# Row maxima of a softmax, transposed on their way to DRAM element by element instead of by TensorE and a VectorE copy

## The reference

```
x = x + layernorm(attention(layernorm(x)))
x = x + layernorm(relu(layernorm(x) @ W1 + b1) @ W2 + b2)
attention: scores = (q * 0.25) @ k^T + mask, softmax over the keys, @ v, then the output projection
```

## Time and profile before

| | us |
|---|---|
| median of 3 runs | 2061.07 (2060.56 to 2062.49) |
| profiled execution | 2061.84 |
| its span | 2060.0 |
| TensorE busy | 1938.2 (94%) |
| VectorE busy | 1536.7 (75%) |
| ScalarE busy | 1408.6 (68%) |
| GpSimd busy | 722.8 (35%) |

### The profile page before, as it was taken

The page is one execution under the profiler, slowest core; times in us unless marked ns, Lnnn a source line. Parts: engine busy times, 40 slices in busy tenths (PEclk is TensorE's granted clock), DMA queues, the critical chain, the costliest instruction groups (busy, mean ns, idle before and its releaser), DMA issues. The chain is left out here.

```text
span 2060.0 us, 70899 instructions
## 1 busy us (share of the span) xinstructions
PE 1938.2 (94%) x27904; PEld 1588.0 (77%) x27904; DVE 1536.7 (75%) x2916; ACT 1408.6 (68%) x2341; POOL 722.8 (35%) x905
## 2 busy tenths in 40 slices
PE   3879999999999999999999999999999999999985
PEld 2557887788888778888877888787788878778765
DVE  6577777777787777778777787877778787777631
ACT  2446677777777777777777776777777677777653
POOL 2013333333333333333333333333433334343343
PEclk8789999999999999999999999999999999999998
DMA  4343343334334333433433343343334334333200
GB/s 124 71 84 73 76 90 68 80 80 93 78 81 91 68 79 81 92 78 82 91 67 77 84 90 79 80 91 66 79 84 88 79 82 89 68 80 76 54 27 16
DMA packets 132817, 160.61 MB, mean 78 GB/s; under 512 B 29408, under 2 KB 82400, under 8 KB 132576
## 3 DMA queue, kind: packets, MB, share of 16 engines
q1 hardware_dynamic: 132048, 156.29, 35.8%
q10 hardware_dynamic: 528, 0.52, 0.1%
HBM read 38.21 MB, written 17.83 MB: 27 GB/s over the span
## 5 line engine op out<-in xcount | busy, mean ns | idle before, releaser
L613 DVE TENSOR_REDUCE max_bias<-p_pair 128x4 f32<-128x1024 f32 (+1 forms) x640 | 761.4, 1215 | 104.1 <-PE p_pair L363 87.9
L530 ACT ACTIVATE probs<-p_pair 128x1024 f32<-128x1024 f32 x640 | 638.8, 1027 | 246.4 <-PE p_pair L363 134.9
L746 POOL TENSOR_TENSOR h_lo<-h_f,h_hi 128x512 fp32r<-128x512 f32 x256 | 329.8, 1288 | 477.5 <-ACT h_hi L562 477.4
L366 PE MATMUL p_pair<-stack 49*128 49x256 f32 (+1 forms) x3072 | 352.3, 314 | 36.3 <-ACT probs L530 15.0
L562 ACT ACTIVATE h_f<-p_pair,b_s 128x256 f32<-128x256 f32 x512 | 247.9, 484 | 119.3 <-PE p_pair L393 119.3
L366 PEld LDWEIGHTS p_pair<-stack 49*128 49x128 f32 (+1 forms) x3072 | 241.3, 191 | 111.6 <-ACT probs L530 46.8
L393 PE MATMUL p_pair<-x_hi,w_hi 64*128 64x256 f32 (+1 forms) x2560 | 302.6, 308 | 13.0 <-DVE x_lo L625 5.5
L393 PE MATMUL p_pair<-w_hi,h_hi 64*128 64x256 f32 x2048 | 286.7, 277 | 10.0 <-POOL h_lo L746 7.4
L393 PE MATMUL p_pair<-x_hi,w_lo 64*128 64x256 f32 (+1 forms) x2560 | 295.9, 302 | 0.0
L393 PE MATMUL p_pair<-x_lo,w_hi 64*128 64x256 f32 (+1 forms) x2560 | 295.7, 302 | 0.0
L393 PE MATMUL p_pair<-w_lo,h_hi 64*128 64x256 f32 x2048 | 284.1, 274 | 0.0
(11 more groups left out here) (77 smaller groups left out, 2815.6 us busy)
## 6 DMA issues: line engine op xcount, KB each, us to landing
stack<-qk SPq DMA_DIRECT2D x1536, 64.0 KB, 2.3
xr<-x SPq DMA_DIRECT2D x32, 512.0 KB, 4.0
out<-yf SPq DMA_DIRECT2D x64, 256.0 KB, 2.2
xa<-x SPq DMA_DIRECT2D x31, 512.0 KB, 4.5
shift_rows<-max_t SPq DMA_DIRECT2D x128, 8.0 KB, 1.3
stack<-shift_rows SPq DMA_DIRECT2D x128, 8.0 KB
probs<-w SPq DMA_DIRECT2D x2, 512.0 KB, 4.9
probs<-w_qkv_t SPq DMA_DIRECT2D x2, 384.0 KB, 5.2
```

The costliest lines, as they stand in the source:

```text
L366: last = nc.tensor.matmul(dst[:, j, col:col + HALF].rearrange("p (a n) -> p a n", a=2), stack[r, stationary, at, kb * P:(kb + 1) * P], two ...
L530: nc.scalar.activation(probs[:, prob_slot(quad, c), :, :], banks("scores", n)[:, :, :], ACT.Exp, scale=SCALE).then_inc(exp_done, 1)
L613: nc.vector.tensor_reduce(dst, src, axis=AX.X, op=ALU.max, negate=True).then_inc(red_done, 1)
L746: nc.gpsimd.tensor_tensor(h_parts[1][:, m:m + 2, :], h_f[:, n % 2, :, :], h_parts[0][:, m:m + 2, :].bitcast(F32), ALU.subtract).then_inc(h ...
```

## The change

The transposes `max_t` and the copies `copy_max` are gone, with SBUF tile `max_t` and four PSUM uses a batch. `store_row` now waits for the five reduces of its quad and stores the 128x16 maxima (`max_q`) straight to the same DRAM scratch with a transposing address pattern, one element of 4 bytes at a time; `load_row` is the same. Each half of `max_q` has its own semaphore for the store, and the first reduce of a quad waits for the store two quads ago.

The tables are new throughout: the full turns have another order, and the first and last turns have tables of their own (`FIRST`, `LAST`) instead of the same table with absent batches left out. In the first turns, x of batch 0 arrives in two halves on two queues, the weights other than qkv are loaded from ScalarE's queue into other tiles and split in five parts (the low parts on GpSimd instead of VectorE), and one of GpSimd's two memsets of `stack` comes before the first LayerNorm, the other waits until it is done.

```diff
-        ("scores_max", 12, -1, 1), ("op", 0, -2, 0), ("max_t", 1, -1, 3), ("scores_max", 13, -1, 1),
+        ("scores_max", 13, -1, 2), ("op", 1, -2, 1), ("scores", 3, -1, 3), ("x1", 0, 0, 2),
...
+FIRST = {
...
+LAST = {
...
                 elif what == "store_row":
...
-                    wait(sp, ev["max_t"], b, QUADS, n + 1)
+                    wait(sp, red_done, b, QC, CH * (n + 1))
                     if not isinstance(b, int) or ready > 0:
                         sp.wait_ge(row_in[n % 2], ready)
-                    sp.dma_start(shift[n % 2], max_t[:, :].bitcast(F32)).then_inc(row_out, 16)
+                    sp.dma_start(shift[n % 2].rearrange("r p -> p r"), max_q[:, n % 2, :],
+                                 allow_slow_non_contiguous=True).then_inc(row_out[n % 2], 16)
                 elif what == "load_row":
                     at = slice(STACK, STACK + ROW + 1, ROW)
-                    wait(sp, row_out, b, 16 * QUADS, 16 * (n + 1))
+                    wait(sp, row_out[n % 2], b, 8 * QUADS, 16 * (n // 2 + 1))
...
-                if what == "max_t":
-                    wait(pe, red_done, b, QC, CH * (n + 1))
-                    last = transposed(dst, lambda r, m: max_bias[r, n % 2, 0:P], 1)
-                elif what == "x1":
+                if what == "x1":
...
                     if c == 0:
-                        wait(dve, mm["max_t"], b, QUADS, quad - 1)
+                        wait(dve, row_out[quad % 2], b, 8 * QUADS, 16 * (quad // 2))
...
-                elif what == "copy_max":
-                    wait(dve, mm["max_t"], b, QUADS, n + 1)
-                    wait(dve, row_out, b, 16 * QUADS, 16 * n)
-                    nc.vector.tensor_copy(max_t[:, :].rearrange("r (j t) -> r j t", j=2),
-                                          banks("max_t", n)[0:4 * KB, :, 0:ROW]).then_inc(ev["max_t"], 1)
...
-            act.dma_start(xa[:, :, :], x_t[0]).then_inc(xa_in, 16)
+            act.dma_start(xa[:, 0:HB, :], x_t[0, :, 0:HB, :]).then_inc(xa_first, 16)
...
+            stack_ones(0)
+
+            def job(what, n, b):
                 half = slice(HB * n, HB * (n + 1))
-                if what.endswith("_rstd"):
+                if what == "ones" and n == 0:
+                    pool.wait_ge(norm_done["ln1"], 2)
+                    stack_ones(1)
+                elif what == "ones":
+                    nc.gpsimd.memset(values[:, :, :], 1.0).then_inc(consts, 1)
+                    pool.wait_ge(consts, 2)
+                elif what == "split_lo":
+                    first_col, stop, stage = W_STAGE[n]
+                    pool.wait_ge(hi_split, n + 1)
```

More of the change, by code:

```diff
@@ L29 @@
[L29 to L34, removed]
@@ L89 @@
+READ = {"scores_max": 20, "scores": 20, "pv": 4, "o_t": 4, "o2": 1, "op": 1, "x2": 1, "f1": 8, "f2": 2,
         "x1": 1, "qk": 4, "v": 1}
 PAIR_OF = {job[:2]: job[3] for job in ORDER["PE"]}
-EVERY = [job for jobs in ORDER.values() for job in jobs]
-AHEAD = max(job[2] for job in EVERY)
-BEHIND = -min(job[2] for job in EVERY)
-LOOP_FROM = BEHIND + 1
 def sandwich(nc, x, w_qkv_t, b_qk, b_v, w_out_t, b_out, w1, b1, w2, b2, ident_in, out):
@@ L228, in opens, with full_turns @@
             return what not in CROSSED or which % 2 == 0
-        def unit_before(what, which, i):
-            jobs = [job for job in ORDER["PE"] if opens(*job[:2])]
-            mine = [job[:2] for job in jobs].index((what, which))
-            for at in range(mine - 1, -4 * len(jobs), -1):
-                name, n, off, pair = jobs[at % len(jobs)]
-                b = i + at // len(jobs) + off
-                if pair == PAIR_OF[what, which] and there(b):
-                    return name, n, b
-            return None
+        def full_turns(engine):
+            offsets = [job[2] for job in ORDER[engine]]
+            return TURNS[0] - min(offsets), NB - max(offsets) - TURNS[1]
@@ new lines, in in_order @@
+        def in_order(engine):
+            start, stop = full_turns(engine)
+            return ([job[:3] for job in FIRST[engine]]
+                    + [(what, n, i + off) for i in range(start, stop) for what, n, off, *_ in ORDER[engine]]
+                    + [(what, n, NB + b) for what, n, b in LAST[engine]])
+        unit_before, last_user = {}, {}
+        for what, n, b in in_order("PE"):
+            if opens(what, n):
+                unit_before[what, n, b] = last_user.get(PAIR_OF[what, n])
+                last_user[PAIR_OF[what, n]] = what, n, b
@@ L241, in reads, with steps @@
         def reads(name, n):
             return (n // 2 + 1) * READ[name] // PRODUCTS[name] if name in CROSSED else n + 1
-        def steps(eng, jobs, job, early=None, unrolled=False):
-            def turn(i):
-                todo = [(what, n, i + off) for what, n, off, *_ in jobs if there(i + off)]
+        def steps(eng, engine, job, early=None):
+            start, stop = full_turns(engine)
+            for what, n, b in FIRST[engine]:
+                job(what, n, b)
+            for what, n, off in ORDER[engine]:
+                job(what, n, start + off)
+            with eng.Fori(start + 1, stop) as i:
+                todo = [(what, n, i + off) for what, n, off in ORDER[engine]]
@@ L251, in turn @@
                 for at, (what, n, b) in enumerate(todo):
-                    if early and not isinstance(i, int):
+                    if early:
                         early(what, todo[at + 1:])
-                    job(what, n, b, i)
-            if unrolled:
-                for i in range(-AHEAD, NB + BEHIND):
-                    turn(i)
-                return
-            for i in range(-AHEAD, LOOP_FROM):
-                turn(i)
-            with eng.Fori(LOOP_FROM, NB - AHEAD) as i:
-                turn(i)
@@ L264, in steps @@
-            for i in range(NB - AHEAD, NB + BEHIND):
-                turn(i)
+                    job(what, n, b)
+            for what, n, b in LAST[engine]:
+                job(what, n, NB + b)
         def two(ap, kb):
```

425 lines of the change are left out of this document (302 added, 123 removed), and 11 rows, old and new, of tables (LAST, ORDER).

## The result

The changed kernel takes 2446.76 us (median of 4 runs, 2436.84 to 2453.91) where the kernel before took 2060.82 beside it: a ratio of 1.187, interval 1.184 to 1.190. It is slower by 386 us; forecast were 2047 us and a range up to 2070. The profiled execution took 2453.91 us, its span is 2452.1.

The account below looks back on a forecast made before the run. TensorE was taken to bound the steady turns (98% busy, 60.1 us each), latency the first batch. 2061.84 - 11 (head) - 3 (steady turns) = 2048, so 2047 us against the median; range 2012 to 2070.

Parts of the forecast that it names:

- T: Landing time of the elementwise store of maxima to DRAM: 3.9 us taken, 1.3 to 7.7 kept as bounds.
- rival 3: Slower: landing over 7.8 us makes SyncE's queue the bound, 4 us a turn per us beyond; 2317 us at 10; chance 0.12.
- (a): SyncE's queue waits for the store's landing before load_row: 45.3 us a turn at 3.9, hidden by TensorE's 60.1.
- (c): Stack loads behind the store in the same rings come later by up to 2.6 us.
- The start: First batch: unblocked LayerNorm pair (6 us) and shorter SyncE hole (5 us) take 11 us off 122.8; first scores near 39.
- The order: Steady turns: new tables give back 0.44 us a turn, 12.8 us in all, by counting PSUM-pair waits; turns of 60.0.
- rival 4: Slower: new order waits 1.2 us more a turn than counted, turns over 61 us; 2082 us; chance 0.1.
- The end: Tail after the last ya: TensorE's last units are the same in the same order, so 75.8 us stay.
- The gain: Removing max_t from TensorE saves 128 x 0.12 = 15.4 us, 0.48 a turn.

Follow-up runs that it names:

- a landing of 4.6 us: Changed kernel with its 4 B elements stored 64 B apart in DRAM, the row read from another tensor after waiting for the store: 2084.31 us, ratio 1.010.
- plain-store kernel: Changed kernel with one line different, maxima stored as 128 rows of 64 B without transposing: 2084.83 us, ratio 1.011.
- old tables: Kernel before with its own tables, transposing unit and copy taken out, maxima stored as 128 plain rows of 64 B: 2050.36 us, ratio 0.994.

## Why the prediction was wrong, point by point

**T, the step that failed.** "Landing is then T = 1.3 + 128 x 0.020 = 3.9 us", with a bound of 7.7. It was 10.5. The 20 ns a descriptor were right (23 measured), the bound of 50 ns was not reached either; what was missing is a second term, 7 us for words that lie 4 B apart in DRAM. The sentence under rival 3, that 16 engines write neighbouring 4 B words of the same rows, pointed at it and then gave it 0.12 for want of a row. The row used as a price counts recorded packets, and these tell nothing of the landing. The Trainium skill's 19 ("DMA: Bandwidth & Descriptors", "Rules for kernel authors") spoke in the right direction; it is against a hardware transpose, which no run here has, and the ratio measured here is 11.1 / 1.4 = 8 against a plain store of the same bytes.

**(a), SP's wait, and rival 3.** At T = 10 it gave 68.8 us a turn and 2317 us; measured are 72.3 a turn and 2447 us. That the size is near is luck, since the mechanism is not the one that the formula holds: with SP's wait gone, 306 of 362 us stay. Term **(c)**, the loads behind the store "later by up to 2.6 us", is the one that was mis-sized: six loads land in 11.7 us and not in 5.5, 6.2 later. Nor did the sum hold PE's 73.8 us of waits for nothing that the profile shows, or the clock, through which an estimated 136 of the 354 us in the middle came. (Two slips in its rows change nothing: twice 17.00 are 34.0, not 34.1, and between scores_max 4 and scores 0 the table has nine score units, not ten.)

**The start.** Its first readings came: the stack's first memset at 0.93, no blocked pair of VectorE, first transposes at 8.53 (forecast 9.3). The second memset doesn't block the split of the weights:

```profile
6.65 0.73 DVE L887 TENSOR_SCALAR xa<-xa,mv_ln,rstd_ln 128x256 f32<-128x256 f32 x2 [0.26 <-POOL rstd_ln L930]
...
8.45 3.51 POOL L906 MEMSET stack<- 32x4096 f32 x1 [0.83 <-DVE xa L887]
...
9.63 1.76 DVE L780 TENSOR_TENSOR w_lo<-probs,w_hi 128x1536 fp32r<-128x1536 f32 x1 [1.25 <-ACT w_hi L713]
```

A VectorE operation with two SBUF inputs runs at 9.63 in 1.76 us beside the memset of 8.45 to 11.96, as long as without it (1.74). The Trainium skill ("SBUF — State Buffer", "Who interferes with whom") says that a VectorE operation with two SBUF inputs contends with a GpSimd operation that reads SBUF, not with one that only writes it; the trace agrees. The 7 us won there were lost again by T: the first row is loaded back at 47.36, the first scores start at 49.55 (before 50.32, forecast 39), and `ya` comes at 127.7. With a landing of 4.6 us the first scores start at 43.55 and `ya` comes at 112.2; with the plain store, which lands sooner, at 44.78 and 114.8. So with a short landing the head gains 8.0 to 10.6 us in these profiles, where 11 were forecast, but the first scores never came near 39: the path to that sum was not the one forecast.

**The order.** Forecast were 60.0 us a turn; with a short landing they are 60.9 in the mean and 61.2 in many turns, about the mark of 61 that was set for rival 4. That step failed as well: "0.44 us a turn comes back" was a count of 15 places against 14. PE's waits in the trace say something else (300 to 1800 us; before, then the plain-store kernel):

```profile
PE p_pair L366 <- ACT probs L530: 8.0, 50, 0.2
PE p_pair L366 <- DVE o_n L652: 4.5, 25, 0.2
```
```profile
PE p_pair L550 <- ACT probs L718: 20.1, 49, 0.4
PE p_pair L561 <- DVE xr L887: 14.6, 24, 0.6
PE p_pair L547 <- DMA stack<-qk: 9.5, 20, 1.0
PE p_pair L550 <- ACT h_hi L750: 8.8, 24, 0.4
PE p_pair L547 <- DVE x_lo L798: 5.6, 24, 0.2
```

All of PE's waits there are 21.9 us before (25 turns, 0.9 each) and 58.6 after (24.6 turns, 2.4 each). Three of these are inputs of a unit (the applied LayerNorm, the stack's load, x_lo), 29.7 us of the 58.6, which the count left out altogether. +1.5 of waits and -0.5 of work are the +1.0.

**The end.** "75.8 us stay": 83.7 with a plain store, 83.8 in the changed kernel. The PE units are the same, 688 or 689, but are busy 52.0 us instead of 47.7, at a clock of 0.79 instead of 0.89. That is 4.3 of the 7.9 us; where the rest comes from, and why the clock is lower, was not sought.

**The gain.** max_t was priced at 15.4 us; with old tables the whole change of path gives 10 in the middle. PE's busy time fell by 18.

Had T been as forecast, the changed kernel would have taken 2084 us, not 2047. That is near rival 4's 2082, but not by its sum alone: the middle is about 29 us longer than at 60.0 a turn, and the end, which rival 4 left at 75.8, another 8.

## What to carry to other kernels

Price a DMA by the time from issue to the wait that it ends, in a trace or by itself, never by its recorded packets; and before an elementwise store to DRAM, ask which elements lie side by side there, and what else runs on the DMA engines in the next 12 us. When TensorE is at 98%, count for each unit of a new order what its inputs wait for as well as its banks, and price the idle time that a change adds twice: as idle, and as matmuls that then run at the lower clock (175 us of idle time came with 179 us of busy time here).

## What the runs showed of the hardware

- 2048 elements of 4 B stored to DRAM: 11.1 us to landing when they lie 4 B apart, 7.8 at 8 B, 5.0 at 16 B, 4.2 to 4.4 from 32 B on; a plain store of the same 8 KB 1.4. The packets of the 2048 elements are recorded within the first 2.5 us whatever the distance.
- Six loads of 64 KB between SBUF tiles take 5.5 us alone, 5.8 beside a store at 64 B and 11.7 to 13.3 beside one at 4 B, from the same or from another queue.
- 2048 descriptors in a store cost 23 ns each on their engine. At 64 B from one to the next, 128 such stores cost the kernel nothing (2084.31 us against 2084.83).
- In the three kernels with the store at 4 B, TensorE stands still for 31 to 74 us in waits for which the profile shows no cause; in the changed kernel all of them end 8 to 12 us after a row store was issued. The others have no such waits.
- TensorE's granted clock has two levels in the traces, 0.50 and 1.00: three pairs of matmuls take 0.64 us at the lower and 0.34 at the upper.
- A gathering load that takes 3.6 us by itself cost the kernel 200 us in 128 uses.
